# The last stage's sums over taps in three groups a pair, and the inner projection in eight 64x32 blocks beside the third

## The reference

```python
r = relu(batchnorm(einsum('bhwc,cd->bhwd', x, Wr) + br))        # x is group-normalised, 16 channels out
w = einsum('bhwd,dk->bhwk', r, Ws) + bs                         # 9 taps for each of 16 groups
xi = einsum('bhwc,cf->bhwf', x, Wi) + bi                        # the inner projection
patches = stack([pad(xi)[:, i:i+H, j:j+W, :] for i in range(3) for j in range(3)])
out = x_in + sum(w * patches, over the taps)
```

## Time and profile before

| | |
|---|---|
| time, median of 3 (lowest to highest) | 784.26 us (782.81 to 785.28) |
| the profiled execution: time, span | 785.05 us, 783.2 us |
| busy, share of the span | TensorE 91%, VectorE 63%, ScalarE 32%, GpSimd 13% |
| mean granted TensorE clock | 0.958 of 2.4 GHz |

### The profile page before, as it was taken

One profiled execution on the slowest core, in us unless ns is written; L12 is line 12 of the kernel. 1 busy time (PEld: TensorE's weight loads), 2 busy tenths in 40 slices (PEclk: granted clock), 3 DMA queues, 4 the chain that ended last, 5 costly groups with the idle time before them and its releaser, 6 DMA issues.

```text
span 783.2 us, 14571 instructions
## 1 busy us (share of the span) xinstructions
PE 712.8 (91%) x6248; PEld 273.4 (35%) x6248; DVE 496.2 (63%) x760; ACT 251.0 (32%) x316; POOL 99.8 (13%) x57
## 2 busy tenths in 40 slices
PE   7427989998999899989979999988999999999994
PEld 7203433332333233323323333323444444444432
DVE  3585745756455554655467668965777777777771
ACT  3722541312312122121200200013554554554532
POOL 2100000000000000000000120212342242242231
PEclk9777999999999999999989999998999999999997
DMA  8940000000000000000000000000111211211212
GB/s 259 165 94 2 1 1 1 2 1 2 1 2 1 1 2 1 1 2 1 2 0 13 2 1 1 2 1 1 28 28 28 54 28 28 54 28 28 51 32 54
DMA packets 55726, 19.59 MB, mean 25 GB/s; under 512 B 52626, under 2 KB 53492, under 8 KB 55540
## 3 DMA queue, kind: packets, MB, share of 16 engines
q1 hardware_dynamic: 55380, 18.58, 10.8%
q10 hardware_dynamic: 288, 0.13, 0.1%
HBM read 10.32 MB, written 8.39 MB: 24 GB/s over the span
## 4 chain that ended last, share of the span: by engine, by line
PE 84%; DVE 11%; ACT 3%; issue 1%; POOL 1%; DMA 0%; ACTq 0%; DVEq 0%; POOLq 0%
PE conv L496 44%; PE att L569 11%; PE conv L552 11%; PE att L532 7%; PE att L393 6%; DVE comb L933 2%; PE att L540 2%; PE conv L369 2%; DVE xpad L922 2%; PE att L413 1%; DVE stats L947 1%; ACT x L631 1%; DVE attn L846 1%; DVE attn L848 1%; PE att L372 1%
## 5 line engine op out<-in xcount | busy, mean ns | idle before, releaser
L496 PE MATMUL conv<-xpad,comb 64*64 64x512 f32 x3456 | 390.3, 601 | 15.3 <-DVE comb L933 11.4
L1108 DVE TENSOR_TENSOR x<-conv,x 128x1024 f32<-128x1024 f32 x144 | 173.0, 1222 | 66.8 <-PE conv L552 66.8
L496 PEld LDWEIGHTS conv<-xpad,comb 64*64 64x64 f32 x3456 | 126.9, 135 | 246.6 <-issue 236.7
L933 DVE SCALAR_TENSOR_TENSOR comb<-experts,wsel,comb 128x576 f32<-128x576 f32 x144 | 107.0, 812 | 73.2 <-ACT comb L652 73.2
L552 PE MATMUL conv<-rstack,wse 98*128 98x512 f32 x288 | 110.1, 479 | 4.5 <-DVE x L1108 2.8
L662 ACT ACTIVATE x<-conv,bias 128x512 f32<-128x512 f32 x64 | 40.6, 685 | 175.4 <-PE conv L496 175.4
L569 PE MATMUL att<-x,sum_sel 64*32 64x512 f32 x1280 | 87.9, 608 | 0.0
L922 DVE SCALAR_TENSOR_TENSOR xpad<-att,x 128x1024 f32<-128x1024 f32 x48 | 56.5, 1219 | 37.0 <-PE att L413 36.8
L552 PEld LDWEIGHTS conv<-rstack,wse 98*128 98x128 f32 x288 | 47.8, 193 | 82.6 <-issue 64.8
L652 ACT ACTIVATE comb<-experts,wsel 128x576 f32<-128x576 f32 x48 | 34.5, 771 | 87.5 <-PE conv L496 80.1
L1175 POOL TENSOR_TENSOR x<-x,xin 128x1024 f32<-128x1024 f32 x16 | 38.2, 2388 | 150.2 <-ACT x L756 150.2
(11 more groups left out here) (117 smaller groups left out, 401.5 us busy)
## 6 DMA issues: line engine op xcount, KB each, us to landing
x<-in_x SPq DMA_DIRECT2D x32, 256.0 KB, 5.2
out<-pixels SPq DMA_DIRECT2D x32, 256.0 KB, 3.2
experts<-in_We SPq DMA_DIRECT2D x2, 576.0 KB
x<-in_c_sum SPq DMA_DIRECT2D x1, 160.0 KB
map_sel<-in_c_map SPq DMA_DIRECT2D x1, 128.0 KB
wr<-in_Wr SPq DMA_DIRECT2D x6, 4.0 KB
x<-in_Ws SPq DMA_DIRECT2D x6, 9.0 KB
ident<-in_c_ident ACTq DMA_DIRECT2D x1, 64.0 KB, 3.2
```

What stands on the lines that cost most here:

```text
L496: last = nc.tensor.matmul(conv[own[to], h, HW * rows:HW * rows + HW], comb[own[rows], q % 2, n, t * C:t * C + C], xpad[own[rows], 2 * (q % ...
L933: v.scalar_tensor_tensor(comb[:, q % 2, n, :], experts[:, e, :], wsel[:, p % 2, j + QP * n, e:e + 1], comb[:, q % 2, n, :], ALU.mult, ALU. ...
L1108: v.tensor_tensor(img(prod[i]), img(conv[:, unit, :]), xip[s][:, kh:kh + H, kw:kw + W], ALU.mult)\
```

## The change

The rounds are issued in three groups a pair: rounds 3 and 4 of the pair before together, behind expansions 0 and 1; rounds 0 and 1 together, behind expansions 4 and 5; round 2 alone, behind expansions 6 and 7. The inner projection moves from behind round 0 to behind round 2. It is made of eight matmuls with weight blocks of 64 rows and 32 columns, each for one image, one half of the pixels and 32 output channels. Its results stand in the quarters of `sum_of`, so that ScalarE copies it out in four pieces of 64 partitions and 512 columns in place of one of 128 and 1024; only the last piece signals. VectorE's and GpSimd's instructions stay as they are.

```diff
-ISSUED_AT = {5: 0, 6: 1, 7: 2}
-ISSUED_LATE = {0: 3, 1: 4}
-R_AT, XI_AT, T_AT = 3, 5, 8
...
+            def project_xi(k, s, m):
+
+                if m:
+                    eng.wait_ge(misc_free, m)
+                eng.wait_ge(xn_ready, k + 1)
+                for n in range(2):
+                    for h, cols in halves():
+                        rows, bank = sum_of(n, h)
+                        for upper in range(2):
+                            last = nc.tensor.matmul(att[rows.start + 32 * upper:rows.start + 32 * upper + 32, 1, bank],
+                                                    wi[own[n], 64 * n + 32 * upper:64 * n + 32 * upper + 32],
+                                                    xn[s][own[n], cols], start=True, stop=True)
+                last.then_inc(misc_full, 1)
...
             def involve(k, s, first=False, last=False):
-                for i in range(TAPS):
-                    expand(k, s, i)
-                    if i in ISSUED_AT:
-                        add_up(k, ISSUED_AT[i])
-                    if i in ISSUED_LATE and not first:
-                        add_up(k - 1, ISSUED_LATE[i])
-                    m = 2 if first else 3 * k + 2
-                    if i == R_AT and not last:
-                        project(k + 1, 1 - s, m, wr[:, :], AR)
-                    if i == XI_AT and not last:
-                        project(k + 1, 1 - s, m + 1, wi[:, :], 128)
-                    if i == T_AT and not first:
-                        turn_back(k - 1, m if last else m + 2)
+                m = 2 if first else 3 * k + 2
+                expand(k, s, 0)
+                expand(k, s, 1)
+                if not first:
+                    add_up(k - 1, 3)
+                    add_up(k - 1, 4)
+                expand(k, s, 2)
+                expand(k, s, 3)
+                if not last:
+                    project(k + 1, 1 - s, m, wr[:, :], AR)
+                expand(k, s, 4)
+                expand(k, s, 5)
+                add_up(k, 0)
+                add_up(k, 1)
+                expand(k, s, 6)
+                expand(k, s, 7)
+                add_up(k, 2)
+                if not last:
+                    project_xi(k + 1, 1 - s, m + 1)
+                expand(k, s, 8)
+                if not first:
+                    turn_back(k - 1, m if last else m + 2)
...
             def empty_xi(s, m):
                 eng.wait_ge(misc_full, m + 1)
-                nc.scalar.activation(xip[s][:, 1:H + 1, 1:W + 1], img(att[:, 1, :]), ACT.Identity, bias=bi_s[:, 0:1])\
-                    .then_inc(misc_free, 1)
+                for n in range(2):
+                    for h in range(2):
+                        rows, bank = sum_of(n, h)
+                        done = nc.scalar.activation(
+                            xip[s][own[n], 1 + 16 * h:17 + 16 * h, 1:W + 1],
+                            att[rows, 1, bank].rearrange("p (a b) -> p a b", b=W), ACT.Identity, bias=bi_s[rows, 0:1])
+                done.then_inc(misc_free, 1)
```

More of the change, by code:

```diff
@@ L573, in involve @@
             def involve(k, s, first=False, last=False):
-                for i in range(TAPS):
-                    expand(k, s, i)
-                    if i in ISSUED_AT:
-                        add_up(k, ISSUED_AT[i])
-                    if i in ISSUED_LATE and not first:
-                        add_up(k - 1, ISSUED_LATE[i])
-                    m = 2 if first else 3 * k + 2
-                    if i == R_AT and not last:
-                        project(k + 1, 1 - s, m, wr[:, :], AR)
-                    if i == XI_AT and not last:
-                        project(k + 1, 1 - s, m + 1, wi[:, :], 128)
-                    if i == T_AT and not first:
-                        turn_back(k - 1, m if last else m + 2)
+                m = 2 if first else 3 * k + 2
[20 more added lines that the diff above has]
+                    turn_back(k - 1, m if last else m + 2)
             project(0, 0, 0, wr[:, :], AR)
-            project(0, 0, 1, wi[:, :], 128)
+            project_xi(0, 0, 1)
             eng.wait_ge(wse_ready, 1)
@@ L599, in _ @@
                 involve(k, k % 2, last=(k == NP - 1))
-            for r in ISSUED_LATE.values():
-                add_up(NP - 1, r)
+            add_up(NP - 1, 3)
+            add_up(NP - 1, 4)
             turn_back(NP - 1, 3 * NP)
```

## The result

The changed kernel takes 817.8 us (median of 4 runs, 816.1 to 818.7) against 784.8 for the kernel before (4 runs). The ratio is 1.042, with a 95% interval of 1.039 to 1.045: 33 us slower.

A forecast was written before the change was run, and what follows sets the result against it. TensorE's own order was taken to bound the kernel. From 784.26 us, 0.60 more in each of 14 pairs, +1.0 and -1.0 at the ends (together +8.4) gave 792.7; six clock falls (9) made it 802, range 787 to 816.

The forecast's parts named there:

- What is saved: TensorE's chain in the last stage: merged groups and small-block projection cut a pair from 14.75 to 13.17 us, 1.58 less.
- VectorE does not take that back: VectorE's products in the last stage fit beside the longer groups: cost nothing, or 0.2 us a pair if not.
- The wait: Turn to pixels waits for ScalarE's four copies of the inner projection: 2.50 us of copies, a stall of 2.18 a pair.
- my upper end: ScalarE's four copies of the inner projection without overlap: 2.8 us.
- my 15.35: One last-stage pair without a clock fall: 13.17 + 2.18 = 15.35 us against 14.75, 0.60 more.
- The clock: TensorE's clock falls to half behind some six of 15 stalls, 1.5 us each: 9 us.
- four in five: Share of TensorE's five waits of 2 us or more between 95 and 500 us that went with a clock fall.
- rival 1: Slow clock behind nearly every last-stage stall, as transposes may not hold it: 814 us, 818 with copies of 2.8; chance 0.27.
- The range: Whole kernel: 787 to 816 us.
- the dearest copies with falls everywhere: Last stage: copies of 2.8 us and a clock fall behind nearly every stall, 818 us; left outside the predicted span.
- +1.0 and -1.0: First pair saves about 1.2 us and stalls 2.18, so +1.0; last pair, without a projection, taken as -1.0.

The follow-up runs named there:

- the better orders: Changed kernel with the eight-block inner projection issued behind rounds 0 and 1, between them, or behind round 0 with rounds 1 and 2 joined later: 765.7, 767.0, 765.6 us.
- the last two orders: Changed kernel with the eight-block inner projection between rounds 0 and 1 (767.0 us), or behind round 0 with rounds 1 and 2 together behind expansions 6 and 7 (765.6 us).
- the first experiment: Changed kernel with the eight-block inner projection issued behind rounds 0 and 1 instead of behind round 2: 765.7 us, ratio 0.978 to the kernel before.

## Why the prediction was wrong

The direction was as predicted, and so were the two mechanisms, a wait for the copies and a half clock that it brings. What failed is the number of falls, and with it the range: the measured 817.8 us stands 1.8 above it. Step by step:

- *What is saved:* 13.17 us for the bare pair. The chain shows the groups at 1.88, and 0.95 for the projection where 0.86 was taken, since its end is now waited for. Right within 0.1.
- *VectorE does not take that back:* right in the changed kernel. In the better orders it does: its product 8 keeps a pair at 13.5 to 13.6.
- *The wait:* the turn waits for the four copies, 14 times, and the small matmul once. Right. Its size was too small. I took 2.50 us for the copies from the middle stage's copy, where two of 0.684 overlap (1.27). Here the four do not overlap: 0.685 each, 0.70 from start to start, 2.78 in all. That was my upper end. The pair without a fall is 15.73 us, 0.38 above my 15.35. The turn starts 2.85 us behind the projection's end and not 2.68, which is 0.17: the copies take 0.28 more, and the handing over before and behind them 0.11 less. The projection is 0.09 dearer. And the turn takes 1.16 us on the empty engine, where the sum had the 1.05 of a turn that follows an expansion (0.89 of the chain and 0.16 of overlap); this 0.11 stood in the sum at nothing. Over 14 pairs the 0.38 are 5 us. The Trainium skill's page (ScalarE: Activation LUTs, "What ACT_TABLE_LOAD costs") has neighbours overlap by 93 ns; the measured four don't, and the measurement decides.
- *The clock:* the step that failed. I expected "a fall behind some six of the stalls" and it came behind 14 of 15. The price was near: 17.08 - 15.73 = 1.35 us, where 1.5 was taken. Eight falls more than expected are 11 us; with the 5 of the wait they make up the 16 between 802 and 818. I had read "four in five" and then gone below it, because most of those gaps were longer; nothing in the rows carried that step. The case was rival 1, for which I had given 814, and 818 with copies of 2.8.
- *The range* left out just "the dearest copies with falls everywhere". That is the case that came. The falls did not need the dear copies, though: with copies of 2.41 us and a gap of 1.92 they came 13 times of 15. That kernel took 811.9 us, inside the range: it took both the copies and the falls to leave it.
- *Why the falls come so regularly* is shown only in part. That the falls of the stalls need the long empty stretch of TensorE is shown: with 0.42, 0.75 and 1.28 us of it there was no fall from 545 us to the last pair, with 1.9 and 2.3 there was one almost each time. It is not the only way to a fall: in the last pair, with gaps of 0.86 and 0.40 us, the clock fell in the traces of the kernel before and of the last two orders, and not in that of the first experiment, which has the same gaps. The rule of the Trainium skill (TensorE: Matmul & The Clock Gate, "Part 4: PE-mode transpose") that I named beside rival 1 is not what made them: with expansions in the transposes' place they came as often, and at 662.56 the clock fell before the first transpose. Whether transposes count for the clock at all no run here shows. Why exactly one stall of the 15 was spared stays open.

In the profiled executions the sum is: from the turn at 561.78 to that at 784.77, 13 pairs take 223.0 us against 13 x 14.75 = 191.8, which is 31.2 more, as much as the span grows (31.1). Of these, 13 x 0.98 = 12.7 are the wait less the saving, and 18.5 the 12 falls in between, one of them of double length. The first and the last pair, for which +1.0 and -1.0 were forecast, come to +0.4 and -0.6.

## What to carry to other kernels

When a producer is moved closer to the one who next needs its buffer, add up what still stands between the two against the whole emptying of that buffer, all its pieces up to the one that signals; here 0.7 us of cover met 2.8 us of copies. A wait on TensorE has a second price when it empties the engine for long: here 1.3 us of slow clock on top of 2.3 us of wait, and about 1 us of matmuls in the gap (with zero weights, or two expansions) avoided it. When a cost has two states, price the pessimistic one together with the upper ends of the other terms, and put that case inside the range.

## What was not expected of the hardware

ScalarE's copies with a bias overlapped when two of 128x512 followed each other (1.27 us for two of 0.684) and did not when four of 64x512 with alternating halves of the partitions did (2.78 for four of 0.685). Matmuls with zero weights held the granted clock as well as real ones: 1.00 throughout, with the same wait for the copies. A turn that starts on an empty TensorE at full clock takes 1.16 us of the chain, and 0.89 when it follows an expansion. With a stall of 2.29 us the falls came in nearly every pair, eight times in a row 17.1 us apart, and not in a share of them.
